# A two-layer gated attention and expert kernel: second attention's first keys inside the last expert tiles, a reordered first prologue, and scatters at other places

## The reference

```python
x = x + tanh(g_xattn[0]) * _L0_xattn_ref(_layernorm(x), ctx_1024, ctx_1024, mask, ...)   # 16 heads of 16, 361 keys, masked
x = x + tanh(g_ffn[0])   * _L0_ffn_ref(_layernorm(x), ...)                               # shared expert + 2 of 8 experts
x = x + tanh(g_xattn[1]) * _L1_xattn_ref(_layernorm(x), ctx_1024, ...)                   # same attention, no mask
x = x + tanh(g_ffn[1])   * _L1_ffn_ref(_layernorm(x), ...)                               # 1 of 8 low-rank experts, width 1024
```

```python
scores = einsum('bhqd,bhkd->bhqk', q, k) / sqrt(16);  attn = softmax(where(mask, -1e15, scores))
ctx = einsum('bhqk,bhkd->bhqd', attn, v);  return ctx @ Wo + bo
```

## Time and profile before

| | before |
|---|---|
| median of 3 runs | 903.62 us (902.23 to 904.96) |
| profiled execution | 903.28 us |
| its span in the trace | 901.4 us |
| TensorE busy | 794.3 us (88%) |
| VectorE busy | 582.5 us (65%) |
| ACT busy | 471.0 us (52%) |
| GpSimd busy | 221.3 us (25%) |
| chain that ended last, by engine | TensorE 61%, DMA 12%, VectorE 10%, issue 7%, SyncE 5% |

### The profile page before, as it was taken

One profiled execution on the slowest core, in us unless ns is written; L12 is line 12 of the kernel. 1 busy time (PEld: TensorE's weight loads), 2 busy tenths in 40 slices (PEclk: granted clock), 3 DMA queues, 4 the chain that ended last, 5 costly groups with the idle time before them and its releaser, 6 DMA issues.

```text
span 901.4 us, 22259 instructions
## 1 busy us (share of the span) xinstructions
PE 794.3 (88%) x7992; PEld 614.1 (68%) x7992; DVE 582.5 (65%) x1773; ACT 471.0 (52%) x1004; POOL 221.3 (25%) x213
## 2 busy tenths in 40 slices
PE   5579999998999987899997689889999999778996
PEld 3346777766676665578985467667677676557996
DVE  4867778776666665675546478778788777463332
ACT  2335556555455545645663156556566565535453
POOL 2535222233332314410007253224212111000000
PEclk9789999999999999999999679999999999879999
DMA  6966778776676741733324958878898875000001
GB/s 186 236 155 163 165 148 176 160 156 139 144 164 148 164 107 34 216 94 107 123 86 112 180 127 173 198 186 176 189 192 161 181 159 97 2 1 1 19 19 37
DMA packets 152379, 119.00 MB, mean 132 GB/s; under 512 B 81020, under 2 KB 143848, under 8 KB 152264
## 3 DMA queue, kind: packets, MB, share of 16 engines
q1 hardware_dynamic: 146656, 109.91, 54.6%
q0 software_dynamic: 4096, 6.57, 2.8%
q10 hardware_dynamic: 1520, 1.12, 0.5%
HBM read 77.84 MB, written 39.46 MB: 130 GB/s over the span
## 4 chain that ended last, share of the span: by engine, by line
PE 61%; DMA 12%; DVE 10%; issue 7%; SPq 5%; ACT 3%; POOL 1%; DVEq 0%; ACTq 0%; POOLq 0%
PE ps L1895 18%; PE ps L2008 8%; PE ps L2034 7%; PE ps L2067 6%; PE ps L2057 5%; DMA cT<-in_ctxT 5%; PE ps L2053 3%; DMA QS<-mp 3%; DMA scr_q<-qp 2%; PE ps L2091 2%; PE ps L2322 2%; DMA QS<-scr_q 2%; DVE mx L1523 2%; DVE ps L1519 2%; SPq L409 1%
## 5 line engine op out<-in xcount | busy, mean ns | idle before, releaser
L965 ACT ACTIVATE prob<-ps 128x400 f32<-128x400 f32 (+1 forms) x384 | 182.6, 500 | 95.9 <-PE ps L2057 88.5
L2034 PE MATMUL ps<-KS,QS 96*100 96x361 bf16 x512 | 168.0, 344 | 24.4 <-DVE mx L1519 9.7
L1519 DVE CUSTOM_DVE_ANT_0 ps<-ps,biasq 100x361 f32<-100x361 f32 x256 | 135.7, 542 | 72.7 <-PE ps L2034 68.9
L1523 DVE TENSOR_REDUCE mx<-ps 100x1 f32<-100x361 f32 x256 | 127.1, 527 | 55.1 <-PE ps L2034 52.5
L2057 PEld LDWEIGHTS ps<-QS,KS 98*128 98x128 bf16 x1536 | 110.2, 101 | 50.8 <-issue 11.2
L2057 PE MATMUL ps<-QS,KS 98*128 98x100 bf16 x1536 | 134.8, 212 | 6.2 <-ACT prob L965 4.5
L2008 PE MATMUL ps<-cT,wk 128*128 128x361 f32 x256 | 103.0, 514 | 16.5 <-DMA ident<-in_ident 9.3
L2034 PEld LDWEIGHTS ps<-KS,QS 96*100 96x100 bf16 x512 | 65.1, 128 | 62.0 <-DVE mx L1519 16.2
L2067 PE MATMUL ps<-prob,V 128*17 128x100 f32 (+1 forms) x3072 | 88.4, 255 | 11.8 <-issue 11.8
L702 POOL TENSOR_TENSOR kp<-kr,kp 128x722 bf16<-128x722 f32 x32 | 48.5, 1517 | 187.2 <-ACT kp L936 187.0
L2067 PEld LDWEIGHTS ps<-prob,V 128*17 128x17 f32 (+1 forms) x3072 | 67.7, 99 | 29.7 <-issue 26.5
(11 more groups left out here) (226 smaller groups left out, 1621.1 us busy)
## 6 DMA issues: line engine op xcount, KB each, us to landing
scr_k<-kp SPq DMA_DIRECT2D x96, 180.5 KB, 5.1
KS<-scr_k SPq DMA_DIRECT2D x64, 270.8 KB
cT<-in_ctxT SPq DMA_DIRECT2D x32, 361.0 KB, 4.5
KS<-scr_k SPq DMA_DIRECT2D x64, 180.5 KB
QS<-scr_q SPq DMA_DIRECT2D x64, 150.0 KB
KS<-scr_k SPq DMA_DIRECT2D x64, 90.2 KB
scr_q<-qp SPq DMA_DIRECT2D x24, 200.0 KB, 3.6
scr_q<-qp SPq DMA_DIRECT2D x48, 100.0 KB, 5.1
```

What stands on the lines that cost most here:

```text
L965: nc.scalar.activation(prob[0:KROWS[t], t, hg, :], ps[0:KROWS[t], c % 2, 0:HQ * S], ACT.Exp).then_inc(a["exp"], 1)
L1519: nc.vector.tensor_tensor_reduce(ps[0:S, banks[h % len(banks)], 0:S2], ps[0:S, banks[h % len(banks)], 0:S2], biasq[p][:, :], 1.0, -3.0e38, ...
L1523: nc.vector.reduce_max(mx[:, h:h + 1], ps[0:S, banks[h % len(banks)], 0:S2], axis=AX.X).then_inc(a["max"], 1)
L2034: mm(ps[0:S, banks[h % len(banks)], 0:S2], QS[p][0:SROWS, h, :], KS[p][0:SROWS, h * S2:(h + 1) * S2], start=True, stop=True).then_inc(a["s ...
```

## The change

It has five parts.

1. **First prologue.** SyncE loads the first group of x first. The first batch's keys and queries are no longer stored and loaded back: `first_keys` and `first_queries` copy the parts from SBUF straight into KS0 and QS0, one DMA for each stack block and half of the heads (24 in all). For that the projection weights are laid out by half of the heads, then dimension, then head, so that a half is one of the two 128-wide outputs. GpSimd no longer fills a row of KS; a 128x128 tile of ones (ident_bf, before it holds the identity) goes to DRAM once, and `restore_rows` fills rows and padding from there. The fills of V1 stand before the start. ACT's queue takes the biases and gates; wo goes to SyncE's. The third and fourth normalized groups move.
2. **Last tiles.** The second attention's keys of batch 0 are projected in item NI - 4, in banks 6 and 7 (`key_bank`), with their parts on ACT and VectorE there and in the next item. TensorE's prologue of the second attention has only values in that place; its pair 1 is transposed and projected between scores.
3. **Second prologue.** Keys of batch 0 are stored and loaded first, the queries are copied directly, and the context of batch 2 is loaded between the two halves of these copies.
4. **Scatters.** GpSimd waits for the weighted sums of step n - 2 instead of its transposed scores, and `SCATTERS` says which of the 32 scatters follow (index i: batch i // 2, choice i % 2).
5. **Weights** of the last layer are loaded in steps 8 to 13 of the second attention.

The diff, cut to its core:

```diff
-KLOADS = len(KRUNS) + 1
+NLOAD = len(KRUNS) + 1
+        SCATTERS = {8: (0,), 9: (1,), 10: (2,), 11: (3,), 12: (4, 5), 13: (6, 7), 14: (8, 9), 15: (10, 11)}
...
+        def key_bank(l, n, m):
+            return (6 if l == 1 and n == 0 else 4) + m
...
+            def first_keys(part, halves):
+
+                a = sa[0]
+                if part == 0:
+                    sp.wait_ge(a["k1"], START + KT)
+                elif part == 1:
+                    sp.wait_ge(a["k2"], START + 1)
+                else:
+                    sp.wait_ge(a["k3"], START + 1)
+                for half in halves:
+                    c = slice(half * HH * S2, (half + 1) * HH * S2)
+                    for r in range(NST):
+                        if KPART[r] == part:
+                            sp.dma_start(KS[0][r * HD:(r + 1) * HD, c], kp[:, part, half, :]).then_inc(sd["kload"][half][0], 16)
+
+            def first_queries(l, half):
+
+                for r in range(NST):
+                    queries_split(l, 0, QPART[r])
+                    sp.dma_start(QS[0][r * HD:(r + 1) * HD, half * HH:(half + 1) * HH, :],
+                                 qp[0][:, QPART[r], half, 0:S]).then_inc(s_fq[half], 16)
...
-                    if l == 1 and b >= 2:
-                        last_weights(b - 2)
+                    if l == 1 and 8 <= b < 12:
+                        inner_weights(b - 8)
+                    if l == 1 and b == 12:
+                        outer_weights(0)
+                        outer_weights(1)
...
                 if l == 0:
+                    x_load(0)
                     ctx_load(l, 0, 0, True)
-                    x_load(0)
+                    mask_load(0, 0, True)
                     x_load(1)
                     ctx_load(l, 1, 1, True)
...
+                if l == 0:
+                    first_keys(0, (0, 1))
+                    x_load(2)
+                    mask_load(1, 1, True)
+                    first_keys(1, (0, 1))
+                    first_keys(2, (0, 1))
+                    x_load(3)
                 else:
-                    pair_store(0)
+                    k_store(l, 0)
+                    for half in range(2):
+                        k_load(l, 0, half)
+                first_queries(l, 0)
+                if l == 1:
+                    ctx_load(l, 2, 0, False)
+                first_queries(l, 1)
...
+            nc.gpsimd.memset(ident_bf[:, :], 1.0).then_inc(s_vones, 1)
...
-                    nc.gpsimd.memset(KS[1][SROWS:KSROWS, :], 1.0).then_inc(s_vones, 1)
...
                         if n >= 8:
-                            pool.wait_ge(sa[0]["sT"], START + 3 * NHG * (n - 1))
-                            scatter(n - 8)
+                            pool.wait_ge(sa[0]["pv"], START + NHG * n)
+                            for i in SCATTERS[n]:
+                                scatter(i // 2, i % 2)
...
-                    for b in range(B - 8, B - 2):
-                        scatter(b)
+                    pool.wait_ge(sa[0]["pv"], START + NHG * (B + 1))
...
             attn(0)
+            for i in range(12, 15):
+                scatter(i // 2, i % 2)
             norm_pair(F0, NPAIR - 1)
-            pool.wait_ge(sn["xn"], START + B * F0 + B)
+            for i in range(15, 20):
+                scatter(i // 2, i % 2)
             for j in POOL_PIECES:
                 low_piece(j)
-            for b in range(B - 2, B):
-                scatter(b)
+            for i in range(20, 2 * B):
+                scatter(i // 2, i % 2)
...
+                    if n == NI - 4:
+                        pe.wait_ge(s_wa[1]["k"], WATTN[1])
+                        pe.wait_ge(s0["xl"], START + NT)
+                        for m in range(KT):
+                            project_k(1, 0, 0, IB, m)
```

417 lines of the change are left out of this document (206 added, 211 removed).

## The result

After takes 897.51 us (median of 7 runs, 894.27 to 900.95), before 903.06 in the same comparison (7 runs, 900.24 to 904.96): 0.994 of it, interval 0.992 to 0.997. That is faster, as forecast, but by 5.5 us and not 23. The profiled executions are 903.28 and 896.48 us, spans 901.4 and 894.3.

| mark | before | after | lead |
|---|---|---|---|
| first step of the first attention | 66.52 | 65.67 | 0.9 |
| maxima turned in step 6 | 182.47 | 181.88 | 0.6 |
| maxima turned in step 14 | 339.81 | 328.17 | 11.6 |
| first shared item | 365.04 | 347.13 | 17.9 |
| first expert rows turned | 392.63 | 386.19 | 6.4 |

The account below looks back on a forecast made before the run. It took TensorE to bound the steady steps, with slack only at the stages' ends. Terms: 903.28 - 10 - 6.5 - 11 - 2 + 5.6 = 879.4, said as 880 us; range 868 to 895.

Parts of the forecast that it names:

- First prologue, 10 us: First attention's start: removing the query store and reload and GpSimd's KS fill wins net 10 us, bounds 5.3 to 14.
- Rival D: First prologue turns SyncE-bound, so only the fill's 5.3 us and 3 us in the second attention are won: 888, chance 0.07.
- The norms' part: First prologue, VectorE: four normalizations take 6.70 us instead of 1.38 beside GpSimd's fill; the 5.3 us go with it.
- Scatters, 11 us: Eight late steps of the first attention: scatters moved behind the weighted sums win 11 of 17.6 us of stalls.
- Rival A: The weighted sums' stalls (L2067) are not the scatters', so only the gate costs: 892 us, chance 0.12.
- Rival E: Slower: scatters start as ACT's copy L951 is released, and uncovered stalls add 30 us: 917, chance 0.04.
- Last step, 2 us: First attention's last step loses its scatters, some of which ran while ACT's copy sat 4.17 us: 2 us won.
- Gate, 5.6 us lost: Before the first expert rows: seventeen scatters instead of four follow the last pair's norm, making the rows 5.6 us late.
- Rival C: The gate is worse: scatters beside VectorE's low pieces lengthen, 7 us more: 887, chance 0.09.
- Keys in the tiles and second prologue, 6.5 us: End of experts to second attention's first step: keys moved into items, queries copied directly, net 6.5 us, bounds 3 to 10.
- Weights, 0: Second attention: moving the last layer's weight loads to steps 8 to 13 changes 0, with 2 us either side.

Follow-up runs that it names:

- e8: After with the third and fourth x loads and the second mask ahead of the 24 direct copies on SyncE: 886.5 us, 1.011 of before.
- e10: After with three SyncE moves in the first prologue (x loads early, eight small loads in step 0, second query store behind the first): 889.4 us, 1.002 of before.
- e6: After unchanged, run again in a comparison where before takes 876.7 us: 890.6 us, 1.018 of before.
- e9: After with GpSimd's third key part run before the wait for the sums and the scatters, not behind them: 894.4 us, 1.012 of before.
- e16: After with e10's SyncE moves, one scatter in each even step and two or three in odd ones: 872.2 us, 0.970 of before.
- e13: After with the second attention's first-batch key projections back in its prologue, queries still copied directly: 894.8 us, 0.989 of before.
- e15: After unchanged, run again as base where before takes 902.2 us: 893.5 us, 0.991 of before.
- e14: After with e10's SyncE moves, scatters as in before, and the keys back in the second prologue: 895.9 us, 0.993 of before.
- e11: After with part 4 undone, so scatters, waits and places are those of before: 886.7 us, 1.004 of before.
- e7: After with GpSimd's wait before the 12 scatters of steps 8 to 15 again for the transposed scores: 884.6 us, 1.009 of before.
- e2: Before with one edit, GpSimd waiting for the weighted sums before the 16 scatters in steps 8 to 15: 885.3 us, 1.009 of before.
- e5: Before unchanged, run again with a profile in another comparison: before 878.2 us, ratio 1.004 to itself.
- e3: After with the last layer's weights loaded at before's steps of the second attention (2 to 8): 890.2 us, 1.018 of before.

## Why the prediction was wrong, step by step

- **First prologue, 10 us: the step that failed.** 0.9 came. "The first half of the queries is there at about 22.1 + 2.5 + 2.0 = 26.6" was 10.7 us short. It took SyncE as free at 22.1, where it was still issuing key copies and x: the sixth query copy was issued at 29.2, not 24.6. And it took the landing of one small copy (1.95 us) for six that stand behind 1.1 MB of others and x: 8.1 us. That the rest would "cost nothing as long as SyncE reaches max_load(0) before the maxima do; counting its issues I find it there about 3 us ahead" was wrong by count (SyncE issues that load at 58.97, 4.2 us after ACT has the maxima) and watched the wrong place: what TensorE came to wait for is the second query store, for whose buffer ACT waits. Rival D named SyncE, at 0.07, and priced it at 4.7. e8 and e10 show that the 10 us were there: 65.9 (e6) to 59.6 and 54.4. The norms' part held: the third and fourth groups took 1.35 and 2.16 us, 4.80 and 6.70 before (the last of these had ended 1.8 us behind the fill, not with it).
- **Scatters, 11 us.** The size came out exactly (11.05), by luck, for the picture did not. Single scatters behind the sums and pairs in odd steps cost little (17.1 to 18.5 us a window); pairs in even steps cost 2 to 3 us, by delaying GpSimd's own work (e9 and e16). I had charged TensorE (L1895) and not asked who waits for what is queued behind the moved scatters. Rival A is refuted: where before breaks up, after's sums run whole, and in the comparison of e13 to e15 they break up in e14, the one with scatters inside them. What makes a scatter hold TensorE on one occasion and not on another (e11) is open. Rival E is refuted too: in the eight steps ACT's copy never waited for a scatter.
- **Last step, 2 us.** 6.3 came (25.2 to 19.0). I had looked at one ACT stall of 4.17 us and counted half of it; the step with no scatters in it is shorter by more than the whole stall.
- **Gate, 5.6 us lost.** 11.5 were. The term counted GpSimd's queue up to the row loads and said that TensorE has nothing else to do then. In the profile TensorE never waited for the rows. It waited 7.7 us for VectorE and lost 4.7 us more on slow matmuls. Two causes stand in the rows: low pieces on top of the last pair's routing (it also happens in e6, where L1363 takes 3.58 us beside them and TensorE waits 1.5), and VectorE and ACT idle while scatters run. Neither has a run of its own. Where sums don't break up the loss is 5 us (33.1 against 28.3 and 27.7; e7, with 36.1, is an exception that I can't explain). That is near what was worked out, but partly by luck: in e6 TensorE waits 2.4 us for VectorE and 1.0 for the rows, at a granted clock of 0.92. Where they do break up, it is 7 to 12. Rival C had 7 more at this place, by scatters that low pieces lengthen; none of the twelve behind them took over 1.0 us.
- **Keys in the tiles and second prologue, 6.5 us.** 4.6 in the profile (6.4 to 11.0), and less where one looks further. The items take 89.1 to 93.0 us in the fifteen profiles with keys in them and 86.8 to 87.2 in four without (before, e2, e5, e14; 88.3 in e13): about 3.4, where 1.3 was charged. The prologue's own gain came: from the last shared item to the turn of the first batch's maxima 38.1 to 39.9 us (before, e2, e5) against 32.0 to 35.7. But step 0 behind it gives it back: 12.6 us in e2 and e5 at a granted clock of 1.00 and 0.99, 16.3 in before at 0.67, 16.4 to 20.6 in the fifteen (0.63 to 0.71 in after, e6, e15 and e16). The forecast ended at the first step and so did not see this. What makes the clock low there was not tested. By e13 the keys' own part is nothing; the share of the direct queries was not isolated.
- **Weights, 0.** Right (e3).
- **The base.** All terms were read from one execution in which the sums broke up. The 17.6 us of stalls belonged to the occasion, not to the kernel alone; where they are absent the change loses 14 us (876.7 to 890.6).

## What to carry to other kernels

When work is moved on one engine's queue, list what stands behind it in the new place and who waits for that; here it was GpSimd's key part and statistics, and ACT's buffer behind SyncE's store. Price a DMA by what is in flight ahead of it, not by the quickest landing of a small one. A stall that nothing in the profile names should be seen in a second comparison before a change is built on removing it. e16 shows a remedy where before takes 898: one scatter ahead of work that is waited for, and more where nobody waits. And a stage's gain should be followed past its end, into the granted clock of the next stage, before it is counted.
